# No barrier behind the first attention, shifts by copies, and a root in nine steps: one transformer block on one core

## The chip, the cores and the metric

The kernel runs on one core of a Trainium2 chip. The metric is the device time of one execution in microseconds (us). The kernel before took 1876.19 us, the median of three runs (1872.53 to 1881.08). TensorE is called PE here, VectorE DVE, ScalarE ACT, GpSimd POOL, and the engine that issues nearly all DMAs SP. Each engine works through its own instructions in the order in which they are written; a wait on a semaphore holds everything that is written behind it on that engine.

## What is computed

Eight sequences of 256 tokens with 128 channels pass through one attention with 8 heads (with rotary positions and a causal mask), and then through a stack of six layers. Each layer has a windowed attention with 16 heads of 64 and a gated feed-forward network. In front of both, half of the channels are shifted by one token. All is float32.

```python
def shift_tokens(t):
    a, s = jnp.split(t, 2, -1)
    s = jnp.pad(s, ((0, 0), (1, 0), (0, 0)))[:, :-1]
    return jnp.concatenate([a, s], -1)
...
        q = l2norm(q) * qs
        k = l2norm(k) * ksc
...
for i in range(DEPTH):
    x = attn_layer(shift_tokens(x), Wqkv[i], q_scale[i], k_scale[i], Wo[i]) + x
    x = ffn_layer(shift_tokens(x), ln_g[i], ln_b[i], W1[i], b1[i], W2[i], b2[i]) + x
...
x = x + ga * _L0_attn_ref(h, L0_attn_wq, L0_attn_wk, L0_attn_wv, L0_attn_wo)
h = _layernorm(x, axis=-1) * (1 + cb) + sb
x = x + gb * _L0_ffn_ref(h, ...)
```

## The kernel before, in words

**First attention.** `first_attention` runs `batch_pe`, `batch_act`, `batch_dve` and `batch_pool` for steps 0 to 9. Step b works on sequence b and on what is left of b - 1 and b - 2, so that steps 8 and 9 only drain. The end of a sequence is `a_residual`, `a_stats2`, `a_root2`, `a_norm2`, `a_modulate2`, which writes its two tiles of `xr`, the stream's activations. Then all four engines meet in `barrier`: each drains, and goes on when all have. Behind it PE writes the banks once (`mark_written`), and DVE sets a row of ones in `gT` and makes the first `rope` table (`scaled_rope`).

**The stream.** A chunk is one sequence of one layer (256 tokens), a pair is two chunks, c and c + 1. There are four pairs a layer and 24 in all, and then `remainder` with the two steps that empty the lag. For pair p the four functions `pair_pe`, `pair_act`, `pair_dve` and `pair_pool` hold one order each, written out by hand or by a planner: work of pair p, the end of chunk c - 1 (the pair before), and the feed-forward network of the pair two before (p - 2). Nothing but this order and the semaphores decides when a step runs.

A chunk goes through these steps. `xt_turn` (PE) brings the activations into the layout with channels on partitions and shifts the upper half: two matmuls against the identity, one against a shifted identity for the first 128 tokens, and two (shifted identity and a corner) for the second 128. `xt_high` (ACT) and `xt_low` (DVE) split the result into two rounded parts. `proj` (PE) makes q, k, v in twelve pieces. `square` (ACT) and `square_sum` (DVE) give the norms of q and k. `rotate_cos` and `rotate_sin` (DVE) and `rotate_add` (POOL) rotate. `norm_step` takes an inverse root of the 64 sums a token has, without the pow operation: steps 0 and 1 on DVE and 2 to 11 on POOL, each of one small instruction that waits for the one before. `normalise` (POOL) multiplies. Then come `turn` and `turn_copy`, `mask`, `scores`, `row_max`, `less_max`, `exponent`, `row_sum`, `row_inverse`, `soft_norm`, `turn_p`, `copy_p`, `values`, `copy_o`, `out_proj` and `out_add`, which adds to `xr`.

The feed-forward network of a pair begins with the shift: `l_shift` (PE, two matmuls into a bank), `l_second` (ACT, from the bank to the upper half of `fx`), `l_first` (POOL, the lower half of `fx`). Then `l_stats` and `l_moments` (DVE), `l_root` (POOL), `l_norm` (ACT), `l_turn` (PE), `l_scale` (ACT), `hidden_gate`, `hidden_a` (PE), `gelu` (ACT), `gated` (DVE), `second_layer` (PE), `m_add` (DVE).

SP's queue has, for each layer, `load_ahead` for the next layer's weights, then `move_values` for every chunk and half (two DMAs each from `v` to `vs`), with `load_out`, `load_norm`, `load_hidden` and `load_second` between them. Behind all pairs DVE does `finish` for four pairs and SP writes them out.

Of the kernel before, what the change touches and what calls it, by code (L numbers as in the profile page):

```python
# [7 lines left out]
F32 = mybir.dt.float32  # L8
# [28 lines left out]
NORM = 12  # L37
ROOM = (1024.0 / 27.0) ** 2
# [8 lines left out]
LAG = 2  # L47

PROJ_BANK = [[6, 1, 4, 7, 0, 4, 1, 2, 1, 0, 7, 6], [2, 5, 1, 3, 4, 5, 7, 1, 7, 2, 7, 3]]
TURN_BANK = [[2, 3, 1, 6, 6, 3, 1, 1], [2, 3, 0, 6, 1, 2, 5, 0]]  # L50
SCORE_BANK = [[2, 0, 3, 1], [5, 2, 2, 5]]
TURNP_BANK = [[0, 7, 4, 6], [3, 3, 4, 1]]
VALUE_BANK = [[0, 7, 1, 0], [3, 7, 4, 4]]
SCORE_BANKS = range(6)
XT_BANK = [6, 7]
OUT_BANK = [6, 6]
SHIFT_BANK, LTURN_BANK, Y_BANK = 7, 3, 6
GATE_BANK = [3, 2, 0]
A_BANK = [5, 4, 2]
# [12 lines left out]
def build(nc, x, wq, wk, wv, wo, Wqkv, q_scale, k_scale, Wo, ln_g, ln_b, W1, b1, W2, b2, c, wmod,  # L72
          eye_in, masks_in, ropeA_in, ropeB_in, out):
    with ExitStack() as ctx:  # L74
# [116 lines left out]
        e_bar = ev("e_bar", 1)  # L191
# [49 lines left out]

        e_wq = ev("e_wq", 1, step=16 * 3)
# [44 lines left out]
        f_sh = past("f_sh", 1)  # L287
        f_xa = past("f_xa", 1)
        f_xs = past("f_xs", 1)
# [16 lines left out]

        def barrier(e, n):
            e.drain().then_inc(e_bar.sem, 1)
            e.wait_ge(e_bar.sem, (n + 1) * 4)
            e.sem_inc(e_hold.sem, 1)  # L310
# [537 lines left out]
        def batch_dve(e, b, on):  # L848
# [16 lines left out]
            if on(b):  # L865
                a_low(e, b)
                if b == 0:
                    fold_low(e)
                    masks(e)
            if on(b - 1):  # L870
                a_max(e, b - 1, 5)
# [45 lines left out]
        def batch_pool(e, b, on):  # L917
# [35 lines left out]
            if on(b):  # L953
# [8 lines left out]
                a_spread(e, b)  # L962
        def first_attention(e, batch):
            for b in range(B + A_LAG):
                batch(e, b, lambda q: 0 <= q < B)
# [6 lines left out]
        def xt_turn(e, l, c):  # L972
# [3 lines left out]
            lo, hi = slice(0, HALF), slice(HALF, M)  # L976
            xc = xr[:, (c % B) * NT:(c % B + 1) * NT, :]
            for t in range(NT):
                e.matmul(o[lo, t * P:(t + 1) * P], xc[:, t, lo], ident, start=True, stop=True)
            e.matmul(o[hi, 0:P], xc[:, 0, hi], down, start=True, stop=True)  # L980
            e.matmul(o[hi, P:T], xc[:, 1, hi], down, start=True, stop=False, skip_group_check=True)
            e.matmul(o[hi, P:T], xc[:, 0, hi], wrap, start=False, stop=True, skip_group_check=True)\
             .then_inc(b_xt.sem, 1)

        def xt_high(e, l, c):
# [3 lines left out]
            e.copy(xsh[:, c % 2, :], banks[XT_BANK[c % 2]][:, 0:T]).then_inc(b_xh.sem, 1)  # L989
# [439 lines left out]
        def pair_pe(e, l, p, on):  # L1429
# [17 lines left out]
            if on(p):  # L1447
                proj(e, l, c, 1)
# [841 lines left out]
```

## Time and profile before

| | |
|---|---|
| median of three runs | 1876.19 us |
| the profiled execution | 1868.75 us |
| its span, first to last instruction | 1867.0 us |
| PE busy | 1732.8 us, 93% |
| POOL busy | 1479.4 us, 79% |
| DVE busy | 1472.2 us, 79% |
| ACT busy | 1404.0 us, 75% |

The profile is one execution. A share of the span is a mean over stages: the first attention takes the first 270 us, the stream the rest, and the last 66 us empty it. Matmuls overlap, and their ends are modelled, so the distance from the start of one to the start of the next says what one costs, and "idle before" says where PE stood still.

### The profile page before, as it was taken

The page shows a single profiled execution, that of the slowest core. Times are in us where ns is not written, and L with a number is a line of the kernel's source. Part 1 is how long each engine was busy: PE and PEld are TensorE (multiplying, and loading weights), DVE is VectorE, ACT ScalarE, POOL GpSimd, SP SyncE. Part 2 cuts the span into 40 slices and gives each one's busy share as a digit, 9 for nine tenths or more (in the row PEclk, how much of TensorE's full clock was granted, in tenths as well). Part 3 has the DMA queues.
Part 4 walks back from the last instruction along what each step waited for, and adds up shares of the span by engine and source line. Part 5 has one row for each costly group of instructions (what it writes and reads, how often), then busy time and mean ns, then how long its engine had stood idle before and what let it go on. Part 6 is the DMA issues. An engine that isn't in the chain of part 4 may idle for free. (4 is left out here: it accounts for less than half of the span.)

```text
span 1867.0 us, 66200 instructions
## 1 busy us (share of the span) xinstructions
PE 1732.8 (93%) x26984; PEld 1428.9 (77%) x26985; DVE 1472.2 (79%) x2952; ACT 1404.0 (75%) x2772; POOL 1479.4 (79%) x1830
## 2 busy tenths in 40 slices
PE   6999967899999999999999999999999999999985
PEld 4788755777778888787887787877778877888773
DVE  5878847778977888888879787888888798889752
ACT  3777744678877888878877877888788878788862
POOL 3777757779888887988888879789888888898860
PEclk9999988999999999999999999999999999999998
DMA  4000011111121111111110211112111101110100
GB/s 140 1 1 1 1 36 34 31 44 32 31 68 44 33 43 32 58 44 42 44 32 22 68 44 43 31 33 67 40 37 44 32 22 41 38 50 22 37 27 23
DMA packets 45485, 70.67 MB, mean 38 GB/s; under 512 B 15476, under 2 KB 28928, under 8 KB 45184
## 3 DMA queue, kind: packets, MB, share of 16 engines
q1 hardware_dynamic: 43712, 64.34, 11.8%
q8 instruction: 216, 3.54, 0.8%
q10 hardware_dynamic: 1472, 2.10, 0.3%
q14 instruction: 85, 0.70, 0.1%
HBM read 21.33 MB, written 1.05 MB: 12 GB/s over the span
## 5 line engine op out<-in xcount | busy, mean ns | idle before, releaser
L1087 POOL TENSOR_TENSOR ra<-ra,rb 128x512 f32<-128x512 f32 x384 | 492.3, 1288 | 116.7 <-DVE rb L1083 111.6
L1132 POOL TENSOR_TENSOR qn<-ra,rs 128x512 f32<-128x512 f32 x384 | 401.3, 1058 | 7.2 <-POOL rs L1125 0.8
L1062 DVE TENSOR_REDUCE ss<-sq 128x8 f32<-128x512 f32 x384 | 260.4, 678 | 91.2 <-ACT sq L1051 91.2
L1214 POOL TENSOR_TENSOR sp<-sp,rl 128x512 f32<-128x512 f32 x192 | 200.0, 1046 | 61.7 <-DVE rl L1209 61.0
L1201 ACT ACTIVATE sp<-sp 128x512 f32<-128x512 f32 x192 | 121.7, 634 | 38.5 <-DVE sp L1196 38.1
L1205 DVE TENSOR_REDUCE sm<-sp 128x8 f32<-128x512 f32 x192 | 128.6, 670 | 15.5 <-ACT sp L1201 13.0
L1179 PE MATMUL pP<-kT,qT 64*32 64x64 f32 x4608 | 106.9, 226 | 2.8 <-issue 2.2
L1179 PEld LDWEIGHTS pP<-kT,qT 64*32 64x32 f32 x4608 | 93.8, 105 | 16.3 <-ACT kT L1152 11.0
L489 POOL TENSOR_TENSOR ra<-ra,rb 128x512 f32<-128x512 f32 x64 | 81.5, 1288 | 29.6 <-DVE rb L485 29.6
L1190 DVE TENSOR_REDUCE mx<-pS 128x8 f32<-128x512 f32 x48 | 32.9, 685 | 91.2 <-PE pP L1179 91.2
L1083 DVE TENSOR_TENSOR rb<-pQ,rope 128x512 f32<-128x512 f32 x144 | 97.9, 680 | 2.9 <-POOL ra L1087 2.9
L1078 DVE TENSOR_TENSOR ra<-pQ,rope 128x512 f32<-128x512 f32 x144 | 96.8, 673 | 0.0
L1051 ACT ACTIVATE sq<-pQ 128x512 f32<-128x512 f32 x144 | 86.5, 601 | 13.2 <-PE pQ L1043 8.6
L1268 PE MATMUL pO<-woB,oT 128*128 128x128 f32 x768 | 95.3, 278 | 0.6 <-DVE sp L1196 0.6
L1268 PEld LDWEIGHTS pO<-woB,oT 128*128 128x128 f32 x768 | 92.9, 195 | 3.0 <-issue 1.0
L555 POOL TENSOR_TENSOR sp<-sp,rl 128x128 f32<-128x128 f32 (+1 forms) x128 | 67.1, 546 | 34.8 <-DVE rl L549 34.6
L337 PE MATMUL pQ<-eye,qn 128*128 128x128 f32 x576 | 88.2, 276 | 4.9 <-POOL qn L1132 2.8
L1268 PE MATMUL pO<-woB,early 128*128 128x128 f32 x768 | 89.8, 275 | 0.8 <-ACT early L1258 0.8
L1248 PE MATMUL pQ<-pt,vs 128*64 128x64 f32 x1152 | 76.4, 228 | 14.8 <-issue 9.6
L1268 PEld LDWEIGHTS pO<-woB,early 128*128 128x128 f32 x768 | 87.6, 192 | 0.9 <-ACT early L1258 0.9
L1258 ACT COPY oT<-pQ 128x512 f32<-128x512 f32 x72 | 42.1, 584 | 53.4 <-PE pQ L1248 53.4
L1248 PEld LDWEIGHTS pQ<-pt,vs 128*64 128x64 f32 x1152 | 66.0, 139 | 21.0 <-issue 18.1
(355 smaller groups left out, 6194.3 us busy)
## 6 DMA issues: line engine op xcount, KB each, us to landing
vs<-v SPq DMA_DIRECT2D x96, 384.0 KB, 3.3
wqkvA<-in_L_ffn_Wqkv SPq DMA_DIRECT2D x18, 512.0 KB, 5.6
vs<-v SPq DMA_DIRECT2D x96, 64.0 KB, 3.0
woB<-in_L_ffn_Wo SPq DMA_DIRECT2D x6, 512.0 KB, 4.2
w<-in_L_ffn_W SPq DMA_DIRECT2D x6, 341.0 KB, 2.9
out<-x SPq DMA_DIRECT2D x4, 256.0 KB, 2.3
x<-in_L_attn_x SPq DMA_DIRECT2D x1, 768.0 KB, 8.1
w<-in_L_ffn_W SPq DMA_DIRECT2D x12, 64.0 KB
```

The costliest lines, as they stand in the source:

```text
L337: return e.matmul(o[:, n * P:(n + 1) * P], y, ident, is_transpose=True, start=(n == 0), stop=True, skip_group_check=True)
L1062: e.tensor_reduce(ss[:, j, :], sq[:, j % 2, :].rearrange("p (h d) -> p h d", d=DB), AX.X, ALU.add).then_inc(b_ss.sem, 1)
L1078: e.tensor_tensor(halves(ra[:, j, :]), r, w, ALU.mult)
L1083: e.tensor_tensor(halves(rb[:, j % 2, :]), r[:, :, ::-1, :], w, ALU.mult).then_inc(b_ab.sem, 1)
L1087: e.tensor_tensor(ra[:, j, :], ra[:, j, :], rb[:, j % 2, :], ALU.add).then_inc(b_ad.sem, 1)
L1132: e.tensor_tensor(qn[:, j % 4, :].rearrange("p (h d) -> p h d", d=DB), ra[:, j, :].rearrange("p (h d) -> p h d", d=DB), rs[:, c % 2, 8 * j ...
L1179: i = e.matmul(o[h][WIN * j:WIN * j + WIN, lo:lo + 2 * WIN], qT[g][r, k, WIN * w:WIN * w + WIN], kT[g][r, k, WIN * w:WIN * w + 2 * WIN], s ...
L1201: e.activation(sp[:, u, :], sp[:, u, :], ACT.Exp, scale=8.0).then_inc(b_ex.sem, 1)
L1205: e.tensor_reduce(sm[:, u, :], groups(sp[:, u, :]), AX.X, ALU.add).then_inc(b_sm.sem, 1)
L1214: e.tensor_tensor(y, y, rl[:, u, :].unsqueeze(2).to_broadcast([P, 8, 64]), ALU.mult).then_inc(b_pn.sem, 1)
L1248: i = e.matmul(o[64 * h:64 * h + 64, t, :, par, :], (v if par else vs)[g][:, t, f:f + 64], pt[:, g, h, 4 * k + 2 * t + par, :, :], start=( ...
L1268: i = e.matmul(o[:, t * M:(t + 1) * M], oT[c % 2][:, k, t * P:(t + 1) * P], woB[:, k, :], start=(k == 0), stop=(k == PAIRS - 1))
```

## The change

It does five things.

1. `barrier`, `mark_written` and the drain steps 8 and 9 are gone. Four new functions `join_pe`, `join_act`, `join_dve`, `join_pool` hold the end of sequence 7 and all of pair 0 in one order for each engine; `stream` begins at pair 1. `scaled_rope` for layer 0 is in step 3 of the first attention. The ones in `gT` are set at the first use.
2. `xt_turn` becomes two plain transposes. The shift is made by the copies out of the bank: `xt_high` and `xt_low` are two instructions each (64 partitions unshifted, 64 partitions with their columns shifted by one).
3. `l_shift` leaves PE and becomes three DMAs in SP's queue (`xr` to `fx`, one partition down); `l_second` is gone; `l_first` goes from POOL to ACT.
4. `norm_step` has nine steps instead of twelve: 0 to 4 on POOL, 5 to 8 on DVE, which are `scalar_tensor_tensor` instructions.
5. All orders and banks of the stream are new. Two moves stand out: `out_add` of chunk c - 1 is near the end of a pair, and `l_stats`, `l_moments` and `l_root` of that pair at the head of the next (before: `out_add` in the middle, `l_stats` at the end); and the turns 0 to 3 and the first scores of chunk c + 1 go to the next pair. `finish` of a pair is called in the last layer and the remainder, two pairs behind.

```diff
-        def barrier(e, n):
-            e.drain().then_inc(e_bar.sem, 1)
-            e.wait_ge(e_bar.sem, (n + 1) * 4)
...
+        def join_dve(e):
...
+            a_residual(e, 7)
+            a_stats2(e, 7)
+            a_norm2(e, 7)
+            xt_low(e, 0, 0)
+            square_sum(e, 0, 0, 0)
...
         def xt_turn(e, l, c):
...
             for t in range(NT):
-                e.matmul(o[lo, t * P:(t + 1) * P], xc[:, t, lo], ident, start=True, stop=True)
-            e.matmul(o[hi, 0:P], xc[:, 0, hi], down, start=True, stop=True)
-            e.matmul(o[hi, P:T], xc[:, 1, hi], down, start=True, stop=False, skip_group_check=True)
-            e.matmul(o[hi, P:T], xc[:, 0, hi], wrap, start=False, stop=True, skip_group_check=True)\
-             .then_inc(b_xt.sem, 1)
+                i = flip(e, o, t, xr[:, (c % B) * NT + t, :])
+            i.then_inc(b_xt.sem, 1)
+
+        def shifted(c, x_):
+            o = banks[XT_BANK[c % 2]]
+            return ((x_[0:HALF, c % 2, :], o[0:HALF, 0:T]), (x_[HALF:M, c % 2, 1:T], o[HALF:M, 0:T - 1]))
...
-            e.copy(xsh[:, c % 2, :], banks[XT_BANK[c % 2]][:, 0:T]).then_inc(b_xh.sem, 1)
+            for dst, o in shifted(c, xsh):
+                i = e.copy(dst, o)
+            i.then_inc(b_xh.sem, 1)
...
+            elif n == FIT:
+                e.scalar_tensor_tensor(p, t, HORNER[0], t, ALU.add, ALU.mult).then_inc(b_rs.sem, 1)
+            elif n < NORM - 1:
+                e.scalar_tensor_tensor(p, p, HORNER[n - FIT], t, ALU.add, ALU.mult).then_inc(b_rs.sem, 1)
...
         def l_shift(e, l, q):
+            it = l * FP + q
             e.wait_ge(b_wx.sem, b_wx.at(l * B + 2 * q + 1))
...
+            e.wait_ge(f_ln.sem, f_ln.at(it - 1))
...
+            e.dma_start(fx[1:P, :, HALF:M], xr[0:P - 1, k:k + FT, HALF:M]).then_inc(f_xs.sem, 16)
+            for b in range(FT // NT):
+                e.dma_start(fx[0:1, b * NT + 1, HALF:M], xr[P - 1:P, k + b * NT, HALF:M]).then_inc(f_xs.sem, 16)
...
         def pair_dve(e, l, p, on):
...
+            if on(p - 1):
+                rotate_cos(e, l, c - 1, 7)
+            if on(p - 2):
+                l_stats(e, l, p - 2)
             if on(p):
                 xt_low(e, l, c)
...
+                square_sum(e, l, c + 1, 7)
+            if on(p - 1):
+                out_add(e, l, c - 1)
+            if on(p):
                 norm_step(e, l, c + 1, 5)
                 norm_step(e, l, c + 1, 6)
                 norm_step(e, l, c + 1, 7)
                 norm_step(e, l, c + 1, 8)
...
         def pair_pool(e, l, p, on):
...
+            if on(p - 1):
+                normalise(e, l, c - 1, 4)
...
+            if on(p - 2):
+                l_root(e, l, p - 2)
...
                 load_out(e, l)
+                if l > 0:
+                    l_shift(e, l - 1, 3)
                 move_values(e, l, 1, 0)
...
                 load_second(e, l)
+                l_shift(e, l, 0)
                 move_values(e, l, 3, 0)
```

At the head of a pair PE's new order is `xt_turn(c)`, turns 0 to 2 of chunk c - 1, `proj(c, 0)`, `xt_turn(c + 1)`, turn 3, `proj(c, 1)`, turn 4, the first scores of c - 1, `proj(c, 2)`, `l_turn`. At its end it is `out_proj(c - 1)` with two `turn_p` inside it, `turn_p(c, 2)` and `turn_p(c, 3)`, the eight `values` of c, `proj(c + 1, 10)`, `proj(c + 1, 11)`.

## Rows read from the trace of the kernel before

**Rows 1.** Windows, each from the first xt_turn of a pair to the next, and the tail

```profile
core 0: us, PE busy (x) PEld busy (x) DVE busy (x) ACT busy (x) POOL busy (x), PEclk, DMA share, GB/s
785.50:849.60 64.10, 61.79 (x1069) 51.33 (x1066) 51.91 (x102) 50.78 (x94) 54.41 (x67) 1.00 0.22 66
849.60:911.00 61.40, 60.88 (x1068) 50.74 (x1065) 51.95 (x100) 50.65 (x94) 52.53 (x65) 1.00 0.15 41
911.00:973.60 62.60, 61.36 (x1067) 51.03 (x1065) 52.23 (x101) 50.64 (x94) 53.40 (x66) 1.00 0.11 32
973.60:1038.90 65.30, 62.45 (x1069) 50.71 (x1066) 56.62 (x105) 53.52 (x100) 56.27 (x66) 1.00 0.11 30
339.90:403.90 64.00, 56.01 (x1029) 46.55 (x1026) 49.69 (x97) 44.13 (x84) 50.55 (x61) 0.97 0.15 39
279.30:339.90 60.60, 44.31 (x672) 33.41 (x669) 41.01 (x74) 31.55 (x59) 45.72 (x55) 0.85 0.13 35
1801.00:1867.00 66.00, 40.64 (x424) 29.21 (x424) 17.58 (x36) 21.42 (x38) 8.07 (x14) 0.82 0.08 24
```

**Rows 2.** PE's timeline, start us and us: an xt_turn, then turns

```profile
595.84 0.28 PE L979 MATMUL pO<-eye,xr 128*64 128x128 f32 x1
...
596.64 0.66 PE L337 MATMUL pQ<-eye,qn 128*128 128x128 f32 x4
597.14 0.60 PE L337 MATMUL pP<-eye,qn 128*128 128x128 f32 x4
597.57 0.60 PE L337 MATMUL pS<-eye,qn 128*128 128x128 f32 x4
```

**Rows 3.** PE's timeline: an l_shift, and two values behind it

```profile
391.17 0.67 PE L1297 MATMUL pM<-xr,eye 128*128 128x256 f32 x2 [0.66 <-issue]
...
391.99 0.34 PE L1248 MATMUL pQ<-pt,vs 128*64 128x64 f32 x4
...
392.97 0.23 PE L1248 MATMUL pM<-pt,vs 128*64 128x64 f32 x2
```

**Rows 4.** Engines' timeline where the first attention ends and the stream begins

```profile
269.98 0.42 DVE L615 TENSOR_TENSOR early<-pO,early 128x256 f32<-128x256 f32 x1 [3.19 <-PE pO L577]
273.24 0.60 DVE L634 TENSOR_SCALAR early<-x,mv,rstd 128x128 f32<-128x128 f32 x2 [1.35 <-POOL rstd L317]
274.82 0.72 POOL L644 TENSOR_TENSOR xr<-early 128x256 f32<-128x256 f32 x1 [0.18 <-POOL early L640]
280.92 0.47 PE L1043 MATMUL pO<-w_high,xsh 128*128 128x512 f32 x1 [0.97 <-DVE xsl L994]
281.70 0.40 PE L1043 MATMUL pQ<-w_high,xsh 128*128 128x512 f32 x1
282.40 0.39 PE L1043 MATMUL pS<-w_high,xsh 128*128 128x512 f32 x1
```

**Rows 5.** Single lines of DVE and ACT: count, ns min/median/max

```profile
L1103 DVE TENSOR_SCALAR sx<-ss x48: 194/330/775, 299.4 to 1783.2; 128x64 f32<-128x64 f32 x48
L994 DVE TENSOR_TENSOR xsl<-pM,xsh x24: 411/414/418, 299.8 to 1759.9; 128x256 fp32r<-128x256 f32 x24
L989 ACT CAST xsh<-pM x24: 373/374/380, 297.8 to 1756.7; 128x256 fp32r<-128x256 f32 x24
```

**Rows 6.** Lines of POOL, 785.5 to 1038.9: busy us, mean ns, idle before

```profile
L1110 POOL TENSOR_TENSOR nt<-nt,sx 128x64 f32<-128x64 f32 x16 | 5.2, 323 | 4.0 <-DVE nt L1107 3.4
```

**Rows 7.** DMA issues by line: KB each, median us to landing

```profile
vs<-v SPq DMA_DIRECT2D x96, 64.0 KB, 3.0
woB<-in_L_ffn_Wo SPq DMA_DIRECT2D x6, 512.0 KB, 4.2
qks<-in_L_ffn_k_scale SPq DMA_DIRECT2D x12, 16.0 KB, 7.4
```

**Rows 8.** The chain that ended last: start us, us, what

```profile
1858.92 0.61 DVE xr L2074
...
1863.53 0.69 DVE x L2077
```

More of the change, by code:

```diff
@@ L1480, in pair_pe @@
             if on(p - 1):
-                out_proj(e, l, c - 2, 1)
+                e.wait_ge(b_tc.sem, b_tc.at(l * B + c - 1, 7))
+                turn_p(e, l, c - 1, 0)
+            if on(p - 2):
+                e.wait_ge(f_G.sem, f_G.at(l * FP + p - 2, 0))
+            if on(p):
+                proj(e, l, c, 8)
+            if on(p - 1):
+                scores(e, l, c - 1, 1)
+            if on(p):
+                e.wait_ge(b_ab.sem, b_ab.at(l * B + c, 4))
+                proj(e, l, c, 9)
+            if on(p - 1):
+                e.wait_ge(b_pc.sem, b_pc.at(l * B + c - 1, 0))
+                turn_p(e, l, c - 1, 1)
+            if on(p):
+                e.wait_ge(b_ab.sem, b_ab.at(l * B + c, 5))
+            if on(p - 1) and not on(p):
+                e.wait_ge(b_tc.sem, b_tc.at(l * B + c - 1, 6))
+            if on(p - 1):
+                out_proj(e, l, c - 2, 0)
                 e.wait_ge(b_pc.sem, b_pc.at(l * B + c - 1, 1))
@@ L1672, in pair_act @@
+            if on(p - 2):
+                gelu(e, l, p - 2, 0)
+                gelu(e, l, p - 2, 1)
+            if on(p - 1):
+                turn_copy(e, l, c - 1, 6)
+            if on(p):
+                square(e, l, c, 4)
+                e.wait_ge(b_ab.sem, b_ab.at(l * B + c, 3))
+            if on(p - 1) and not on(p):
+                e.wait_ge(b_tc.sem, b_tc.at(l * B + c - 1, 4))
+            if on(p - 1):
                 mask(e, l, c - 1, 2)
-                turn_copy(e, l, c - 1, 6)
@@ L1800, in pair_dve @@
             if on(p - 1):
-                row_sum(e, l, c - 1, 1)
-                row_inverse(e, l, c - 1, 1)
+                rotate_sin(e, l, c - 1, 7)
+            if on(p - 1) and last(p - 1):
+                scaled_rope(e, l + (p - 1) // FP + 1)
+            if on(p - 2):
+                l_moments(e, l, p - 2)
             if on(p):
@@ L1815, in pair_dve @@
             if on(p):
-                square_sum(e, l, c, 3)
+                rotate_cos(e, l, c, 7)
             if on(p - 1):
@@ new lines, in pair_dve @@
+            if on(p - 2):
+                m_add(e, l, p - 2)
+            if on(p):
+                row_sum(e, l, c, 1)
+                row_max(e, l, c, 2)
+                row_inverse(e, l, c, 1)
+                less_max(e, l, c, 2)
+                row_max(e, l, c, 3)
+                less_max(e, l, c, 3)
+            if on(p) and last(p):
+                split_low(e, l + 1, 1, 0)
+            if on(p):
+                row_sum(e, l, c, 2)
+            if on(p) and last(p):
+                split_low(e, l + 1, 1, 1)
@@ L2019, in pair_pool, with stream @@
                 normalise(e, l, c + 1, 3)
-                soft_norm(e, l, c, 2)
-                soft_norm(e, l, c, 3)
-        def stream(e, pair):
-            for p in range(FP):
+        def stream(e, pair, after=lambda p: None):
+            for p in range(1, FP):
                 pair(e, 0, p, lambda q: q >= 0)
```

1295 lines of the change are left out of this document (821 added, 474 removed).

## The prediction, made before the changed kernel was run

> **What bounds the kernel now.** I read the page's busy times first, then the windows of single pairs, then PE's timeline inside a pair, and last the two ends of the stream. The page (the table above) says PE 93%, and the other three 75 to 79%. The windows say it for the stage that matters: four pairs of one layer take 64.1, 61.4, 62.6 and 65.3 us, and PE is busy for 61.8, 60.9, 61.4 and 62.5 us of them [rows 1]. PE idles 2.3, 0.5, 1.2 and 2.8 us, 1.7 us in the mean. The busiest other engine, POOL, has 53 to 56 us, and DVE 52 to 57 [rows 1]. So in the steady stream, 22 pairs from 403.9 to about 1801 us, PE is the bound, and a microsecond taken from PE's work is worth nearly one as long as no other engine or chain comes up to it. The clock of PE is at its full level there (1.00). It is otherwise at the ends: pair 0 takes 60.6 us with PE busy 44, pair 1 takes 64.0 with 56, and the 66 us of the tail have 41 [rows 1]. There the kernel waits for chains, not for an engine.
>
> **Part 1, PE's work.** An xt_turn is the way from 595.84 to 596.64, 0.80 us [rows 2]. A turn is four transposes and takes 0.43 us (597.14 to 597.57 [rows 2]), so two transposes take 0.22 us. A chunk saves 0.58 us, a pair 1.16. An l_shift goes from 391.17 to 391.99, 0.82 us, of which its start may hold a little of the wait before it [rows 3]; I take 0.75. Together 1.9 us a pair. In 22 steady pairs that is 42 us. If PE's idle time of 1.7 us a pair stays, this is the gain; that it stays is the choice here, since the order is wholly new. It can shrink to none (22 x 1.7 = 37 us more) or grow.
>
> **Part 2, what the other engines get.** POOL loses five of its ten root steps a chunk, each 0.32 us and some 0.08 us to the next [rows 6], so ten a pair, 4 us, and the copy `l_first`. It falls to some 49 us. ACT gets one more cast for each chunk (0.37 us [rows 5]), and swaps `l_second` for `l_first`, which are alike: from 50.7 to 51.5. DVE gets one more half of `xt_low` a chunk (at most 0.41 us [rows 5]), 0.8 a pair, and eight small root instructions a pair instead of four. The trace has no `scalar_tensor_tensor` of 64 columns on DVE. The nearest row is step 0, of the same size, with 0.19 us at best, 0.33 in the middle and 0.78 at worst [rows 5]. Eight of them are 1.6 to 6.2 us, where the four of before took 1.0 (two like the middle, two like the best). I take 2.2. So DVE goes from 52 to 54 us, bounds 53.4 to 58, and in a layer's last pair from 56.6 to 58.6, bounds 58 to 62.6. PE's new work is 60.9 - 1.9 = 59.0 us. DVE thus stays under PE in three pairs of four, with little room in the fourth.
>
> **Part 3, two new waits on DVE.** Steps 5 to 8 wait for POOL's steps 0 to 4, which wait for the last `square_sum`. Five POOL steps at 0.40 are 2.0 us. For chunk c three large DVE instructions stand between (0.6 us each), which cover 1.8. For chunk c + 1 only `out_add` does (0.35), so DVE waits about 1.6 us. The second wait is `l_stats`, for the shift's DMAs. These are issued when `out_add(c - 1)` is done. Between that and `l_stats` DVE has the 1.6 us of waiting, four steps of 0.25 and one `rotate_cos` of 0.6: 3.2 us. Three DMAs are issued one behind the other, some 0.5 us each, and the nearest row, the small one of `move_values`, also from SBUF to SBUF, lands 3.0 us after its issue [rows 7]. So the last lands at about 4.0 us. DVE waits 0.8 us. With 1.6 + 0.8 it comes to 56.4 us in an ordinary pair, still below 59.
>
> Who waits behind `l_stats`: `xt_low(c)`, and with it `proj(c, 0)` on PE. From the end of `out_proj(c - 1)` PE has two `turn_p` (0.87), eight `values` at 0.49 (two in 391.99 to 392.97 [rows 3]: 3.9), two projections at 0.70 (281.70 to 282.40 [rows 4]), the new xt_turn 0.22 and three turns 1.3: 7.7 us. `out_add` ends some 1 us after `out_proj`, so 6.7 us are left, and the chain needs 4.0 + 0.8 (four statistics) + 0.7 (xt_low) = 5.5. It is hidden with 1.2 us of room. Put as a limit: a landing later than 5.2 us after `out_add` costs PE. The same chain goes on through `l_moments`, `l_root` and `l_norm` to `l_turn`, in front of which PE has another turn, projections and scores; it has a little more room there. At a layer's edge `load_out` sits right ahead of `l_shift` in SP's queue, with 512 KB and 4.2 us [rows 7]. A shift behind it can land 1 to 2 us later; I count 1 us for each of five layers, 5 us lost.
>
> The Trainium skill, DMA: Bandwidth & Descriptors, Anatomy of one DMA, gives a DMA a fixed cost of about 2.0 us and the bytes over 436 GB/s. By it this shift (130 KB) would land after some 2.3 us and not 3.0, the room would grow and the sum would stay. Its section Specifications says that pieces below 512 bytes are read, modified and written, and the shift consists of 508 pieces of 256 bytes; that speaks against the change. What the trace shows of such pieces stands with the last rival.
>
> **Part 4, the join.** The last result of the first attention is ready for DVE at 269.98; `a_norm2` ends at 273.84; POOL's last instruction ends at 275.54; the barrier, the bank writes and the table follow, and the first projection starts at 280.92 [rows 4]. In the new order the transpose of sequence 0 needs nothing from sequence 7 but the bank that `a_residual` frees, and the only thing ahead of `xt_low(0, 0)` on DVE is `a_norm2`. 273.84, four small memsets and two halves of `xt_low` (0.8) give about 275. So 6 us. Pair 0 then took 60.6 us in a filtered full order, with POOL busy 45.7 and DVE 41.0 [rows 1]. Its new order has less in it (no turns of chunk 1, five steps of the root less for each chunk), and POOL's work falls to about 40. With its start of some 6 us until POOL is fed, I take 50: 10 us. It can't be below 46, and if the order is no better it saves 3. Pair 1 takes 64.0 with no engine above 56; I take 59, of which the 1.9 us of part 1 are a piece: 5 us, bounds 2 and 9.
>
> **Part 5, the tail.** Four `finish` stand in a row behind the last `m_add`, from 1858.92, one every 1.3 us, the last starting its second half at 1863.53 [rows 8]. Three go ahead: 4 us. The turns, scores and softmax of the last chunk's first half come later than before, but run beside the second half, which was the later one anyway; bounds 0 and 5 us lost. The shift by DMA in place of PE's queue gains some 1 to 2. Together 5 us won.
>
> **Sum.** 42 - 5 + 6 + 10 + 5 + 5 = 63 us. The profiled execution took 1868.75 us with a span of 1867.0, so 1806. The median of the three runs lies 7.4 us above it, and the measure is the median: 1876 - 63 = **1813 us**.
>
> **Rivals.**
> *A, the forecast:* 1813. The terms' bounds (landing, join 6 to 20 us, tail 0 to 8) give 1795 to 1830.
> *B, the new order also removes PE's idle time.* The four pairs of a layer differ by 3.9 us in length but by 1.6 in PE's busy time [rows 1], so some of it is order and not work. All of it gone: 1813 - 37 = 1776. Against it: DVE's slack shrinks from 9 us to 3 a pair.
> *C, DVE or the chain at the head of the pair becomes the bound.* If the small instructions take the upper end (58 us) and the two waits are added (2.4), an ordinary pair is 60.4, a last one 65, and with some idle time left the pair stays at 63.3. The 42 us are gone, the ends stay: 1876 - 21 = 1855.
> *D, it doesn't do what it says:* the barrier covered a chain that is there without it, the new join is no shorter, and PE's savings fall into waits: 1873.
> *E, slower: the shift's landing.* The `qks` loads, with pieces of 128 to 256 bytes, land after up to 7.4 us [rows 7]. They come from HBM, which speaks against a transfer, and `move_values` has pieces of 2 KB, so neither row is the same. A landing of 8.5 us after `out_add` holds PE 8.5 - 5.2 = 3.3 us a pair, and DVE 5 us. 22 x 3.3 = 73 us against 63 gained, and 1886; with what POOL then lacks, 1890. It decides from a landing of 8.1 us on.
>
> **How the numbers follow.** A 0.50, B 0.15, C 0.20, D 0.05, E 0.10. The range leaves out D and E and reaches into B and C: 1768 to 1862. A measurement of this kernel can tell 0.5% from no change, 9.4 us. Faster by more than that: A, B and C, 0.85. Within it: D, 0.05. Slower: E, 0.10.
>
> **What the changed profile would show.** Windows of a pair 1.5 to 2.5 us shorter in the same layer, with PE still over 96% busy, DVE at 53 to 57 us and POOL near 49 (part 1 and 2). `l_stats` waiting for a DMA by under 1 us, and no wait of PE for `xsl` in steady pairs (part 3). The first projection of the stream near 275 us, and the next pair's xt_turn near 325 (part 4). One `finish` behind the last `m_add` (part 5). I am wrong if PE waits for DVE or for `l_norm` at each pair's head (C or E), if the small instructions on DVE take over 0.5 us each (C), or if the join's pair takes over 58 us.

## The result

| | before | after |
|---|---|---|
| median of the runs compared | 1874.36 us | 2022.26 us |
| lowest to highest | 1869.43 to 1881.08 | 2015.92 to 2027.63 |
| the profiled execution, its span | 1868.75, 1867.0 us | 2027.63, 2025.8 us |

The ratio is 1.0785, with a 95% interval of 1.0738 to 1.0833: 148 us slower, where 63 us faster was forecast. The time lies outside the range, on the other side. The traced execution of after is the slowest of its four, so the traces differ by more (159 us) than the medians. One execution among all that follow, in experiment 10, ran at a granted clock of 0.75 and took 2128 us; the ratios leave it out.

**The profile after.** Three lines of its page's costliest groups say most of it. The columns are the group, its count, the busy time and the mean ns of one, and then the idle time of the engine ahead of it with its releaser.

```profile
L1422 PE MATMUL pS<-w_high,xsh 128*128 128x512 f32 x144 | 85.9, 596 | 112.7 <-DVE xsl L1373 87.0
L1689 DVE BATCH_NORM_STATS2 fst<-fx 128x6 f32<-128x128 f32 x96 | 20.9, 280 | 153.6 <-DMA fx<-xr 153.6
...
L1495 DVE SCALAR_TENSOR_TENSOR nt<-nt 128x64 f32<-128x64 f32 x48 | 61.6, 1284 | 54.2 <-POOL nt L1493 54.2
```

`l_stats` (L1689) holds DVE for 153.6 us, waiting for the shift's DMAs, 24 times. Behind it PE waits for `xt_low` (L1373) at the pair's first projection (L1422). The first matmuls of that projection take 596 ns in the mean, where [rows 4] have 390 to 470; most of this is not the clock, for experiment 1, with the clock back, still has 553. And one of the root's small instructions (L1495) takes 1284 ns, not some 230.

The windows (columns as in [rows 1]) are the join's pair, the next one, all 21 pairs up to the last one's start, and the last part of the tail:

```profile
273.50:335.10 61.60, 38.35 (x512) 29.63 (x512) 43.62 (x85) 30.62 (x57) 38.81 (x43) 0.86 0.11 31
335.10:395.50 60.40, 53.64 (x1006) 44.77 (x1004) 51.40 (x94) 45.08 (x86) 47.62 (x51) 0.97 0.14 36
...
395.51:1871.79 1476.28, 1303.45 (x21927) 1078.04 (x21925) 1176.47 (x2254) 1099.70 (x2027) 1054.30 (x1145) 0.95 0.14 38
...
1941.00:2025.80 84.80, 49.58 (x582) 34.06 (x582) 23.41 (x51) 30.36 (x52) 17.67 (x21) 0.79 0.10 27
```

The same 21 pairs of the kernel before, start of the third to start of the last:

```profile
404.63:1738.38 1333.75, 1293.45 (x22346) 1069.83 (x22345) 1116.27 (x2127) 1078.23 (x1984) 1135.74 (x1376) 1.00 0.14 41
```

So the third pair starts 9.1 us earlier than before (395.5 against 404.6), the 21 pairs take 142.5 us more (70.3 us each, not 63.5), and from the last pair's start to the end it is 154.0 us against 128.6. The sum, -9.1 + 142.5 + 25.4, is the 158.8 us between the spans. The granted clock is at its half level for 150.2 us of the 21 pairs, against 3.4 before. (All such sums are from the clock's own records in the traces.)

One pair's boundary shows how. This is the timeline of after (start us, us, engine, line, instruction, idle before):

```profile
810.63 0.42 DVE L1646 TENSOR_TENSOR xr<-pM,xr 128x256 f32<-128x256 f32 x1
811.21 0.72 SPq L1672 DMA_DIRECT2D fx<-xr  x1
811.97 7.58 SPq L1674 DMA_DIRECT2D fx<-xr  x2
...
812.80 1.28 POOL L1466 TENSOR_TENSOR ra<-ra,rb 128x512 f32<-128x512 f32 x1
812.87 1.29 DVE L1495 SCALAR_TENSOR_TENSOR nt<-nt 128x64 f32<-128x64 f32 x1 [1.82 <-POOL nt L1493]
...
818.27 0.63 PE L334 MATMUL pP<-eye,qn 128*128 128x128 f32 x4 [0.37 <-POOL qn L1507]
...
821.90 0.87 DVE L1689 BATCH_NORM_STATS2 fst<-fx 128x6 f32<-128x128 f32 x4 [6.35 <-DMA fx<-xr]
...
823.63 0.77 PE L1422 MATMUL pS<-w_high,xsh 128*128 128x512 f32 x1 [4.73 <-issue]
824.19 0.63 PE L1422 MATMUL pS<-w_low,xsh 128*128 128x512 f32 x1
```

`out_add` (L1646) ends at 811.05. The shift's large DMA is issued at once; SP is then held with the two small ones until 819.55, and the data is there only at 821.9, 10.8 us after `out_add`. The prediction put 4.0 us there, its limit at 5.2 and rival E's point at 8.1. The other boundaries are like it: in all 24, `l_stats` starts 10.7 to 11.7 us after `out_add`, the highest five at a layer's edge, behind `load_out`. PE stands still for 4.73 us and then goes on at 630 to 770 ns a matmul where [rows 4] have 390 to 470, at 1.2 GHz and not 2.4.

The DMA view of 811 to 822 (the window in 40 slices: mean share of the 16 DMA engines in tenths, and GB/s) says why it lasts that long:

```profile
DMA  0000000002000000001000000000000101009969
GB/s 0 0 0 0 0 6 15 17 11 74 17 16 19 18 19 18 18 19 47 16 16 15 16 15 16 16 16 15 16 16 15 17 16 16 16 4 343 283 164 313
```

A steady 16 GB/s, with about a tenth of the engines' time in use: 127 KB as 508 pieces of 256 bytes, one every 16 ns, for 8.1 us. The engines do 164 to 343 GB/s right behind it, for `move_values`. So the pieces went one behind the other. That a single DMA engine moved them is inferred; the trace kept here doesn't name the engines. The Trainium skill, DMA: Bandwidth & Descriptors, section Why a DMA increments its semaphore by 16 and not by 1, gives the rule: the number of engines is the largest up to 16 that divides the slowest dimension of both sides, so that 127 partitions all go to one. The trace agrees as far as it tells, and so does experiment 1, where the same pieces are cut into 112 and 15 partitions. I had not weighed this rule.

### The profile page after: what moved, and what is told of

The parts are those of the page before. It is cut to its first block and busy times, and to the rows that moved or that the text cites. A ratio compares the mean times of both kernels' runs of the same rounds, so it can differ in the third digit from the quotient of the medians.

```text
span 2025.8 us, 65232 instructions
## 1 busy us (share of the span) xinstructions
PE 1742.3 (86%) x26499; PEld 1436.2 (71%) x26499; DVE 1543.5 (76%) x3101; ACT 1431.4 (71%) x2822; POOL 1388.9 (69%) x1566
## 5 line engine op out<-in xcount | busy, mean ns | idle before, releaser
L1422 PE MATMUL pS<-w_high,xsh 128*128 128x512 f32 x144 | 85.9, 596 | 112.7 <-DVE xsl L1373 87.0
L1689 DVE BATCH_NORM_STATS2 fst<-fx 128x6 f32<-128x128 f32 x96 | 20.9, 280 | 153.6 <-DMA fx<-xr 153.6
L1549 PE MATMUL pT<-kT,qT 64*32 64x64 f32 x4608 | 113.0, 229 | 18.2 <-issue 10.1
L1422 PEld LDWEIGHTS pS<-w_high,xsh 128*128 128x128 f32 x144 | 29.9, 207 | 131.0 <-issue 127.1
L1549 PEld LDWEIGHTS pT<-kT,qT 64*32 64x32 f32 x4608 | 97.2, 107 | 29.5 <-issue 24.5
L1430 ACT ACTIVATE sq<-pM 128x512 f32<-128x512 f32 x120 | 72.3, 602 | 60.4 <-PE pM L1422 58.4
L1602 ACT COPY pt<-pP 64x512 f32<-64x512 f32 x96 | 55.9, 582 | 70.8 <-PE pP L334 70.2
L1495 DVE SCALAR_TENSOR_TENSOR nt<-nt 128x64 f32<-128x64 f32 x48 | 61.6, 1284 | 54.2 <-POOL nt L1493 54.2
L334 PE MATMUL pO<-eye,qn 128*128 128x128 f32 x576 | 98.0, 298 | 1.4 <-ACT kT L1527 1.0
L1638 PE MATMUL pM<-woB,early 128*128 128x128 f32 x768 | 93.5, 275 | 0.8 <-DVE xr L1792 0.8
L1638 PEld LDWEIGHTS pM<-woB,early 128*128 128x128 f32 x768 | 91.2, 192 | 3.4 <-DVE xr L1792 1.0
```

The lines of the kernel that those rows point to most:

```text
L334: return e.matmul(o[:, n * P:(n + 1) * P], y, ident, is_transpose=True, start=(n == 0), stop=True, skip_group_check=True)
L1422: i = e.matmul(o, x_[:, c % 2, t * P:(t + 1) * P], w[:, kind, g * CH:(g + 1) * CH], start=(k == 0), stop=(k == 2))
L1430: e.activation(sq[:, j % 2, :], banks[PROJ_BANK[c % 2][n]], ACT.Square).then_inc(b_sq.sem, 1)
L1549: i = e.matmul(o[h][WIN * j:WIN * j + WIN, lo:lo + 2 * WIN], qT[g][r, k, WIN * w:WIN * w + WIN], kT[g][r, k, WIN * w:WIN * w + 2 * WIN], s ...
L1638: i = e.matmul(o[:, t * M:(t + 1) * M], oT[c % 2][:, k, t * P:(t + 1) * P], woB[:, k, :], start=(k == 0), stop=(k == PAIRS - 1))
```

## The experiments

Numbers are medians; ratios are to the kernel before, run beside it, with 95% intervals. "Busy" and "idle" are PE's, over the 21 pairs as in the window above.

### Experiment 1: the large DMA in two

```diff
-            e.dma_start(fx[1:P, :, HALF:M], xr[0:P - 1, k:k + FT, HALF:M]).then_inc(f_xs.sem, 16)
+            for lo, hi in ((0, 112), (112, P - 1)):
+                e.dma_start(fx[lo + 1:hi + 1, :, HALF:M], xr[lo:hi, k:k + FT, HALF:M]).then_inc(f_xs.sem, 16)
```

> The changed kernel with one edit: the shift's large DMA of 127 partitions is cut into one of 112 and one of 15. Theory (the 127 rows go through a single DMA engine, 508 pieces one behind the other at 16 ns, so that the shift lands 10.8 us after out_add and holds DVE 6.4 us a pair, and PE behind it): the landing falls to 4 to 5 us, DVE's wait for fx from 154 us to under 25, PE's clock goes back to 1.00 in the stream, and the time to 1860 to 1900 us. Rival (the new order itself is slow: softmax of the odd chunk deferred, root on two engines): DVE's wait falls but other waits come in, and the time stays above 1960.

Measured: 1871.59 us, ratio 0.9999 (0.9977 to 1.0020). Same bytes, same pieces, one DMA more, and 151 us are gone. DVE's wait for the shift fell from 153.6 us to 23.1, the half-level clock in the 21 pairs from 150.2 us to 10.2. In the 21 pairs PE's idle time fell by 96.7 us and its busy time, with the same matmuls, by 48.1. The wait for the landing and the clock behind it are the whole loss against the kernel before. What is left is a kernel equal to the one before, not 63 us faster. (Its traced execution is the fastest of ten, 10 us under the median.)

### Experiment 2: the same DMAs, the small ones first

```diff
-            e.dma_start(fx[1:P, :, HALF:M], ...)
             for b in range(FT // NT):
                 e.dma_start(fx[0:1, b * NT + 1, HALF:M], ...)
+            e.dma_start(fx[1:P, :, HALF:M], ...)
```

> The changed kernel with the shift's two small DMAs issued ahead of the large one of 127 partitions. Theory (one engine moves all 127 rows): nothing but the order of issue changes, the rows still take 8 us, DVE's wait for fx stays at 6 to 6.6 us a pair, time 2010 to 2030. Rival (it is the issue of the small ones, 6.9 us behind the large one in the queue, that costs): the three are issued within 2 us, the landing falls to under 6 us, DVE's wait to under 2 us a pair, and the time to about 1900.

Measured: 2065.49 us, one execution, 35 us above what the theory gave and far from the rival's 1900. DVE waits longer, and the time grows with the wait:

```profile
DVE fst L1689 <- DMA fx<-xr: 194.6, 24, 10.3
```

41 us more than the 153.6 of after, and 43 us more in time. That SP was held behind the large DMA was not the price; the large DMA's own landing is. It is now issued 1.2 us later, behind the two small ones, and `l_stats` starts 12.5 us after `out_add` instead of 10.8.

### Experiment 3: GpSimd's large addition ahead of the root

```diff
+                rotate_add(e, l, c, 6)
                 norm_step(e, l, c, 0)
...
                 norm_step(e, l, c, 4)
-                rotate_add(e, l, c, 6)
```

(on top of experiment 1, for both chunks and in the join)

> As the split shift, and POOL does rotate_add(6) ahead of root step 0 instead of behind step 4, so that POOL is idle while DVE does steps 5 to 8. Theory (the first small instruction on DVE, 1.28 us in each of 48 cases, stands still for as long as POOL's rotate_add of 1.29 us runs, which starts with it): it falls to 0.23 us, DVE gains 2 us a pair, POOL's wait for the root grows from 1.0 to about 1.2, and the time is 5 to 30 us under the split shift's. Rival (1.28 us is what an instruction with the same tensor as both inputs costs): it stays at 1.28 us, and the time is equal or higher.

Measured: 1857.35 us, ratio 0.9940 (0.9919 to 0.9962), 14 us less than experiment 1, and the first kernel here that beats the one before. Its line for the root's fifth step, and its timeline where that step stands:

```profile
L1495 DVE SCALAR_TENSOR_TENSOR nt<-nt 128x64 f32<-128x64 f32 x48 | 10.8, 225 | 87.1 <-POOL nt L1493 87.1
```

```profile
862.28 0.38 POOL L1493 TENSOR_SCALAR nt<-nt 128x64 f32<-128x64 f32 x1
862.70 0.23 DVE L1495 SCALAR_TENSOR_TENSOR nt<-nt 128x64 f32<-128x64 f32 x1 [1.12 <-POOL nt L1493]
862.95 0.48 DVE L1497 SCALAR_TENSOR_TENSOR nt<-nt 128x64 f32<-128x64 f32 x2
```

The instruction is unchanged, and takes 225 ns instead of 1284. In after, GpSimd's addition started at 812.80, the small one on DVE at 812.87, and both ended within 0.1 us of each other. That it reads one tensor twice is not the reason. DVE's wait for GpSimd ahead of it grew from 54.2 us to 87.1, so of the 51 us that DVE no longer works 33 are waiting; the 14 us are what the new order gives in all. The Trainium skill, SBUF — State Buffer, section SBUF: two separate sides, describes it: GpSimd and a DVE instruction with two inputs in SBUF share a pair of ports by an exclusive lock, and whoever comes second stands still until the first is through. The trace agrees to 0.1 us.

### Experiment 4: part 2 of the change alone, in the kernel before

```diff
-            (xt_turn's five matmuls)
+            for t in range(NT):
+                i = flip(e, o, t, xr[:, (c % B) * NT + t, :])
...
-            e.copy(xsh[:, c % 2, :], banks[XT_BANK[c % 2]][:, 0:T]).then_inc(b_xh.sem, 1)
+            for dst, o in shifted(c, xsh):
+                i = e.copy(dst, o)
```

> The kernel before with part 2 of the change alone: two plain transposes for the five matmuls, and the shift in the copies. Theory (PE bounds the stream of the kernel before, and a chunk saves 0.58 us of it): 24 pairs by 1.16 us, 28 us less, ratio 0.985 (0.980 to 0.990). Rival (the saved PE time falls into waits, as ACT and DVE get one instruction more for each chunk at the head of the pair's chain): no change within 0.3%, or slower.

Measured: 1940.44 us, ratio 1.0379 (1.0359 to 1.0400), 68 us slower, where I had priced it as a gain. Two instructions of 367 ns stand where one of 375 to 395 stood on ACT, and on DVE two of 0.42 us where one of 0.41 to 0.42 stood. The next runs take it apart.

### Experiments 6 and 7: the two halves of that, each alone in the kernel before

Experiment 6 halves the evictions and keeps the five matmuls:

```diff
-            e.copy(xsh[:, c % 2, :], banks[XT_BANK[c % 2]][:, 0:T]).then_inc(b_xh.sem, 1)
+            for r in (slice(0, HALF), slice(HALF, M)):
+                i = e.copy(xsh[r, c % 2, :], banks[XT_BANK[c % 2]][r, 0:T])
+            i.then_inc(b_xh.sem, 1)
```

> The kernel before with nothing changed but that the eviction of the turned chunk and its remainder are each two instructions over 64 partitions instead of one over 128; same values. Theory one, the two-instruction evictions are the whole of the 68 us that part two alone cost in the old order: 1935 to 1965. Theory two, the transposes did it (their place, their clock, what follows them on the tensor engine): 1874 to 1895, at most 0.8 us a pair.

Experiment 7 has the two transposes with whole evictions, and leaves the attention's shift out:

> The kernel before with two transposes in place of the five products and whole evictions, one instruction each; the shift of the attention's columns is left out. Theory one (the halved evictions cost): this is before less some 0.5 to 1 us of tensor engine a pair: 1850 to 1874. Theory two (the transposes cost): 1930 to 1945, as with the halved evictions.

Measured: 1912.98 us, ratio 1.0228 (1.0186 to 1.0270), and 1906.36 us, 1.0168 (1.0127 to 1.0210). 40 us and 34 us slower. Neither theory had this: both halves cost, and they add up to the 68. In experiment 6 the 21 pairs take 20.9 us more; another 15.7 us of the trace's 36.5 lie ahead of them, 5.7 in pair 0 and 7.1 in pair 1. In the 21 pairs PE waits for `xt_low` at the pair's first projection, 13.0 us in 21 waits, which the kernel before did not:

```profile
PE pO L1047 <- DVE xsl L997: 13.0, 21, 0.7
```

In experiment 7 nothing became longer, PE has 334 matmul records less, and the order is the old one. PE's busy time falls by 1.7 us, its idle time rises from 40.3 to 79.5. Most of the rise stands inside `scores` (L1174), 28.5 us in 17 waits against 2.2 in one before, and the profile names nothing that ended these waits:

```profile
PE pP L1174 <- issue: 12.0, 6, 2.7
PE pQ L1174 <- issue: 9.4, 6, 2.5
...
PE pT L1174 <- issue: 5.2, 4, 1.7
```

The DMA records show what they have in common. Queue q8, named "instruction", brings a piece of 16 KB 176 times in these 21 pairs (179 in the kernel before, whose PE has more instructions). Every one of PE's 34 gaps over 0.25 us without a releaser, 46.7 us, ends 2.1 to 3.1 us after such a piece starts; only 13% of the time lies so. In the kernel before there are 16 such gaps, 16.6 us, and again all end there. So 30 of the 39 us of new idle time look like PE waiting for its own code. No run changes the code's place alone, so this is an inference, and why the gaps fall more often into `scores` here stays open.

Its clock falls to the half level in seven stretches, 23.9 us in all, where the kernel before has one:

```profile
406.30:1777.56 1371.26, 1291.78 (x22012) 1063.23 (x22011) 1117.03 (x2127) 1076.33 (x1985) 1134.43 (x1375) 0.99 0.14 39
...
806.40:809.80 3.40, 3.24 (x36) 2.68 (x37) 2.50 (x5) 1.46 (x3) 0.00 (x0) 0.50 0.11 24
```

Ahead of the stretch shown PE had stood still for 2.70 us, to 806.56, in one of those gaps. The 20.5 us more at the half level cost some 10 us in this trace. The granted clocks of all executions differ less, 0.978 in the mean against 0.981, or some 6 us.

### Experiment 5: the attention's shift back on PE, in the new order

Experiment 5 is experiment 3 with before's `xt_turn`, `xt_high` and `xt_low`:

> The kernel of the third experiment (1857.4 us) with the attention's shift back on the tensor engine: five products a chunk in place of two transposes, and each eviction of the turned chunk again one instruction instead of two. Theory one, the halved evictions are what costs (0.74 and 0.84 us a chunk where one took 0.39 and about 0.45, with the tensor engine idle behind them): each of two chunks a pair gives back 0.8 us and pays back some 0.7 us of matmuls, some of it hidden: 1820 to 1855. Theory two, the matmuls that the change took out were the gain, as my part one had it (1.1 us a pair for this half of it): 1880 to 1890.

Measured: 1872.08 us, ratio 1.0000 (0.9983 to 1.0017), 15 us slower than experiment 3. It lies between the two theories. In this order the matmuls that the change took out were a gain, smaller than theory two had it: PE's busy time grows by 27.3 us, of which some 9 are the clock (27.3 us at its half level against 10.2), and its idle time falls by 8.9.

### Experiment 8: the twelve-step root, in the new order

Experiment 8 is experiment 3 with before's root, all twelve steps on GpSimd behind `rotate_add(e, l, c, 6)`:

> The third experiment's kernel (1857.4 us) with the root of before, twelve steps, all on GpSimd at the place of the first five. Theory, as my part two had it: seven more steps of some 0.44 us on GpSimd against four of 0.23 us on the vector engine and two handings over, so 1.5 to 2.0 us more in a chain on which the first normalised rows wait, twice a pair; it shows in part: 1880 to 1940. Rival: GpSimd's slack covers it, 1855 to 1866.

Measured: 1929.38 us, ratio 1.0301 (1.0280 to 1.0322), 72 us slower, inside what the theory gave. The nine-step root is worth 3 us a pair here. PE's busy time is unchanged but for 7 us; its idle time is 123.4 us against 70.4. The wait that grew is the expected one, PE's for `normalise` at the turns, 62.5 us against 3.9. Two of the twelve steps stood on DVE in the kernel before, so this is somewhat more than the root of before.

### Experiments 9 to 12: small edits of the order

Experiment 9, on top of 3, makes the two small DMAs one:

```diff
-            for b in range(FT // NT):
-                e.dma_start(fx[0:1, b * NT + 1, HALF:M], xr[P - 1:P, k + b * NT, HALF:M]).then_inc(f_xs.sem, 16)
+            e.dma_start(fx[0:1, 1:FT:NT, HALF:M], xr[P - 1:P, k:k + FT:NT, HALF:M]).then_inc(f_xs.sem, 16)
```

> The kernel of the third experiment (1857.4 us) with the shift's two small DMAs as one, so three issues of about 0.6 us instead of four. In its trace the shift's landing still holds DVE's l_stats 20 times of 21, 1.2 us in the mean (25.4 us), and PE's l_turn waits 17.6 us for l_norm at the end of that chain. Theory, the landing is the start of what holds l_turn: the last landing comes 0.6 us earlier, DVE's wait falls to 12 to 15 us, PE's to about 8, and the time by 6 to 12 us: 1845 to 1852. Rival, l_turn's wait has another cause and the wait only moves: 1856 to 1858.

Experiment 10, on top of 3, puts the four `finish` at the end:

> The third experiment's kernel with the four finish steps behind all pairs again, as in the kernel before: part five of the prediction, undone alone. Theory, as predicted: three more of them stand behind the last m_add, 1.3 us each, 4 us, 1861.5. Rival: the writes out hide them or they disturb the last pairs by as much when early: 1857 within 1.

Experiment 11, on top of 9:

```diff
+                rotate_sin(e, l, c, 7)
                 norm_step(e, l, c, 5)
```

> The kernel with three DMAs, and on DVE rotate_sin of chunk c's last piece ahead of the four root steps instead of behind them. DVE stands idle there for POOL's fifth step (74 us in 42 waits, both chunks), so 0.6 us of work fits into each of 21 waits: up to 12 us of DVE's time. Theory one, DVE's order is what holds the pair now: 5 to 12 us less than the kernel with three DMAs. Rival, these waits are slack: within 1 us of it.

Experiment 12, on top of 11, moves `l_turn` behind `proj(e, l, c, 3)`:

> The kernel with the filled wait and l_turn one projection (1.2 us) later in PE's order. If PE's waits for l_norm (up to 1.8 us, 17.6 us in 16) are a real hold, they vanish and up to 8 us are gained over the kernel with the filled wait. Rival: the feed-forward network's chain behind l_turn is as tight, and what PE no longer waits for there it waits for at hidden_gate: within 2 us, or some us slower.

| | median us | ratio, 95% |
|---|---|---|
| 9, three DMAs | 1856.18 | 0.9933 (0.9914 to 0.9953) |
| 10, finish at the end | 1865.91 | 0.9971 (0.9955 to 0.9986) |
| 11, filled wait | 1861.73 | 0.9953 (0.9936 to 0.9971) |
| 12, l_turn later | 1856.96 | 0.9939 (0.9917 to 0.9960) |

Experiment 9 took DVE's wait for the landing from 25.4 us to 4.9, as meant, and gained nothing. PE's wait for `l_norm` stayed at 16.4 us (17.6), so the landing is not what it comes from; DVE's own wait moved to `xt_high` on ACT, behind `l_stats`, from 10.7 us to 27.9:

```profile
DVE xsl L1373 <- ACT xsh L1363: 27.9, 20, 1.9
...
PE pS L334 <- ACT early L1718: 16.4, 15, 1.8
...
DVE fst L1689 <- DMA fx<-xr: 4.9, 7, 1.4
```

Experiment 11 took 14 us from DVE's wait for the root (72.8 to 59.2) and gained nothing either; it is 5.6 us above 9, outside both of its expectations, with intervals that overlap. Experiment 12 removed PE's wait for `l_norm` wholly, and two others took its place, 7.3 us for `xt_low` and 10.3 for `l_scale`; it shows no gain over 3 or 9, and its time is 5 us under 11 with intervals that overlap. Experiment 10 is 0.3% slower than 3, with intervals that touch, and its trace has 137.2 us from the last pair's start to the end instead of 133.0, the 4 us that were priced.

### Experiments 13 to 15: one long chain out at a time

All three are experiment 3 with work left out. Experiment 13 has whole evictions and leaves out the attention's shift:

> The third experiment's kernel (1857.4 us) with whole evictions of the turned chunk, one instruction each on ACT and DVE; the shift of the attention's columns is left out. In the old order the halving alone cost 40 us. If the head of the pair is what turns freed work into idle time here too, 25 to 40 us less: 1817 to 1832. If the new order covers it, within 5 us: 1852 to 1858.

Experiment 14 copies `fx` whole on ACT and leaves out the network's shift and its DMAs:

> The third experiment's kernel with the feed-forward network's input copied whole by ACT and no shift DMAs; the shift of these columns is left out. DVE's wait for the landing (25 us) and, if the chain behind it is what holds PE's l_turn, its 17.6 us go: 1835 to 1845. If the landing is covered, as the three-DMA kernel suggests: 1850 to 1858.

Experiment 15 leaves out the root's steps on DVE:

```diff
-                e.tensor_scalar(t, t, -1.0, None, ALU.add).then_inc(b_rs.sem, 1)
+                e.tensor_scalar(rs[:, c % 2, :], t, -1.0, None, ALU.add).then_inc(b_rs.sem, 1)
```

> The third experiment's kernel with the root cut after its fifth step, whose result is used as it is; the four steps on DVE (0.23 us each, 48 times, 43 us of DVE's work) and the hand-over to DVE and back are left out. If the hand-over (DVE waits 74 us in 42 waits for the fifth step, GpSimd 50 us for the ninth) is what holds the pairs: 20 to 50 us less, 1807 to 1837. If it is slack: 1850 to 1857.

Measured: 1845.21 us, ratio 0.9872 (0.9829 to 0.9915); 1858.75 us, 0.9921 (0.9896 to 0.9946); 1860.26 us, 0.9932 (0.9907 to 0.9956). The first lies between its two expectations: the halved evictions cost 12 us in the new order (0.7%, give or take 0.5), less than the 40 of the old one. The shift's landing, once the DMA is cut, costs nothing that can be measured when it alone is left out. Nor do DVE's root steps, though DVE waited 87 us for the step ahead of them. But these two waits stand side by side: without the root's steps DVE waits 107.4 us for the landing, where experiment 3 has 28.4, and without the landing it still waits 85.8 us for the root. No run left out both.

```profile
L1685 DVE BATCH_NORM_STATS2 fst<-fx 128x6 f32<-128x128 f32 x96 | 20.9, 281 | 107.4 <-DMA fx<-xr 107.4
```

The windows of 3 and 15:

```profile
393.87:1718.61 1324.74, 1254.36 (x21927) 1040.30 (x21925) 1131.29 (x2254) 1091.74 (x2026) 1057.41 (x1144) 1.00 0.15 43
```

```profile
391.12:1726.35 1335.23, 1254.14 (x21927) 1047.38 (x21925) 1099.45 (x2089) 1090.33 (x2027) 1055.36 (x1144) 0.99 0.15 43
```

32 us less of DVE's work in 15, the same of PE's, and the pairs are 10 us longer, with the clock at its half level for 23.9 us against 10.2.

## Why the prediction was wrong, point by point

PE over the 21 pairs, from the windows. "Behind code" is the part of the idle time in gaps over 0.25 us without a releaser that end 2.1 to 3.1 us after a piece of 16 KB on queue q8 starts.

| kernel | length | busy | idle | behind code | clock at half |
|---|---|---|---|---|---|
| before | 1333.8 | 1293.5 | 40.3 | 16.6 | 3.4 |
| 6, before, halved evictions | 1354.6 | 1301.8 | 52.8 | 16.0 | 3.4 |
| 7, before, transposes | 1371.3 | 1291.8 | 79.5 | 46.7 | 23.9 |
| 4, before, both | 1395.9 | 1292.4 | 103.5 | 51.6 | 20.5 |
| after | 1476.3 | 1303.5 | 172.8 | 33.6 | 150.2 |
| 1, shift in two DMAs | 1331.4 | 1255.3 | 76.1 | 32.4 | 10.2 |
| 3, addition ahead of the root | 1324.7 | 1254.4 | 70.4 | 31.4 | 10.2 |
| 8, twelve steps | 1385.2 | 1261.7 | 123.4 | 35.9 | 30.7 |

Each row is one execution. "Busy" is no pure measure of work: experiment 6 has the matmuls of before and 8 us more of it.

Of the 209 us between the forecast and the result, 151 are the landing (after against experiment 1), and 59 are what the rest of the forecast had wrong.

**Part 3, the failed step.** The landing was taken from the small row of `move_values` in [rows 7], 3.0 us, as "the nearest row, also from SBUF to SBUF", and put at 4.0 for the last of three. It measured 10.8. That row moves 32 partitions, this DMA 127, and 127 was the number that set its time, not the size of the transfer. Nor was it the pieces of 256 bytes, which the prediction weighed: experiment 1 has the same pieces. With the measured value the prediction's own limit gives 10.8 - 5.2 = 5.6 us a pair, 123 in 22. The pairs grew by 6.9 against experiment 1: 4.6 of PE's idle time and 2.3 of its busy time. That the clock would fall behind such a wait stood nowhere in the prediction. The limit itself was too strict, by an estimate of 1 us: in experiment 1 the last of the four DMAs lands 5.2 us after `out_add` in the mean (4.1 to 6.3), `l_stats` starts at 5.7 (median), and PE waits for `xt_low` for 6.1 us in the whole kernel.

Rival E had the place and the limit, but not the mechanism. Its 8.5 us came from loads with pieces of 128 to 256 bytes, and the size of the pieces was not the cause. That it pointed the right way was in part luck. Its chance of 0.10 was too small, and so was its end: with its 1890 in the range the result would still lie 130 us outside.

The 2.3 us worked out from the Trainium skill, DMA: Bandwidth & Descriptors, Anatomy of one DMA, are close to the 2.4 that the DMA of 112 partitions shows. But that section is on DMAs that GpSimd issues, and this one is issued by SP; for the DMA as it was the same sum was 8 us off. In experiment 3 the four DMAs land 2.2 to 2.5 us after their issue (medians), so the 3.0 was near for each of them. What was short is the time from the first issue to the last: all four take 2.9 to 3.4 us to issue. DVE's wait is 25.4 / 21 = 1.2 us there, where 0.8 was forecast.

**Part 1, the work right, the time wrong.** 1.9 us a pair less of PE's work was forecast. Experiment 3 has 59.7 us a pair against 61.6: 1.87. (The 59.0 in part 2 is taken from the pair with the least work, not from the mean.) But its idle time is 3.35 us a pair against 1.92, so of 39.1 us that PE no longer works, 30.1 came back as waiting, and 9.0 were gained. Of the 30.1, 14.8 are gaps behind code. "If PE's idle time stays, this is the gain" was named as the choice, and it did not stay. 93% busy said that PE is the fullest engine. It did not say that PE's order waits for nothing; experiment 7 takes only PE's work away from the old order and is 34 us slower.

**Part 2, the small instructions.** A `scalar_tensor_tensor` of 64 columns takes 225 ns when alone, near the 330 ns I took, and 1284 ns when GpSimd's addition stands beside it, over the upper bound of 0.78 us. To free the two a pair that were held gave 14 us, with the change of order that it took (experiment 3 against 1). DVE's busy time in experiment 3, 53.9 us a pair, is the forecast 54, and GpSimd's, 50.4, near the 49. What I priced too low is the root: 4 us a pair off GpSimd was counted as room only, and experiment 8 shows 72 us. The halved evictions I counted by DVE's and ACT's busy time. They stand in the chain in front of the pair's first projection, and cost 12 us in the new order. In the old one they cost 40, of which 21 are in these 21 pairs.

**Part 4, the join.** 21 us were forecast, 9.1 measured, 10.8 in experiment 3. The first projection is at 277.60 against 280.92, 3.3 us of the 6, since `a_norm2` ends at 276.35 in after and not at 273.84. The chain up to it is as long as before; its start, `a_residual`, is at 272.50 and not at 269.98. That start differs from one execution to the next: experiment 1, with the same first attention, has it at 270.46, and experiment 4, with the old one, at 271.27. The join's pair takes 61.6 us, not 50, and not less than the 60.7 of pair 0 before. GpSimd is busy for 38.8 us in it, near the 40 forecast, and PE for 38.4. No engine has over 44, so its length is that of a chain and not of work; which chain was not looked at. The clock is 0.86, as before. The pair behind takes 60.4, against a forecast of 59.

**Part 5, the tail.** The early `finish` is worth about what it was priced at: 4.2 us in the traces, 0.3% or 6 us by the ratios, give or take 5 (experiment 10). But the tail as a whole is 133.0 us against 128.6 (experiment 3), so 8.6 us are lost beside it, where the bound said 0 to 5 and the sum had nothing. That half of a chunk's turns and scores now come a pair later is the likely reason; no run takes it apart.

**The rivals.** Without the long landing, D and C come nearest: experiment 1 lies at 1872, where D said 1873, and experiment 3 at 1857, where C said 1855. D's "PE's savings fall into waits" holds for three quarters of them; what it said of the join does not, since 9.1 us were gained there. C's reason, DVE as the bound, is not what the runs show: 32 us less of DVE's work changed nothing.

**Still open** is a part of what holds PE for those 3.35 us a pair. Taking out the landing, the root's steps on DVE, a part of DVE's wait or PE's wait for `l_norm` each moved idle time elsewhere, and no run took out two of them together. But 1.5 us a pair, 31.4 of the 70.4 us, are gaps that wait for no other engine: 29 of the 30 gaps without a releaser end 2.1 to 3.1 us after a piece on the instruction queue starts. One of experiment 3, from its timeline, and the DMA view of 792.2 to 794.9, in which nothing else moves:

```profile
794.76 0.21 PE L1549 MATMUL pP<-kT,qT 64*32 64x64 f32 x1 [1.84 <-issue]
```

```profile
DMA packets 1, 0.02 MB, mean 6 GB/s; under 512 B 0, under 2 KB 0, under 8 KB 0
q8 instruction: 1, 0.02, 2.0%
```

Such a gap doesn't end on another engine's work, which fits that shortening the waits between engines gained nothing. So it is not only the order and the semaphores that decide when a step runs here. The join was not undone by itself; its gain is read from the traces.

## What to carry to other kernels

Before a shift or any odd slice goes to a DMA, count the partitions of both sides: 127 rows took 8.1 us to move, and as 112 and 15 they landed 2.4 and 2.5 us after their issue; where the trace has no row for a new transfer that something waits for, put the longest row of its kind into the range. In a kernel of hand-ordered engines a full engine is not the same as an engine that sets the time: work taken from it is a gain only after the order has been made for it, and a run with that one edit alone tells which it is. Where the profile names nothing that ended a gap, look whether a piece on the instruction queue came just ahead of its end.

## What was not expected of the hardware

- The DMA of 127 partitions, 508 pieces, goes at 16 ns a piece and 16 GB/s, and the queue's next DMA is held: of the 7.58 us for the two small ones behind it 6.9 are the first one's, 0.6 the second's. With 112 + 15 partitions, all four take 2.9 to 3.4 us to issue.
- A DVE instruction of 0.23 us took 1.28 beside a GpSimd one of 1.28 that had begun 0.07 us earlier.
- Halving an eviction by partitions halves nothing: 64 x 256 takes 367 ns on ACT and 0.42 us on DVE, 128 x 256 takes 375 to 395 ns and 0.41 to 0.42.
- With fewer matmuls and the shift left out (experiment 7), PE's gaps without a releaser grew from 16.6 us to 46.7, all ending 2.1 to 3.1 us after a 16 KB piece on the instruction queue began, and the clock was at 1.2 GHz for 23.9 us instead of 3.4 in the traces.
